# Depthwise taps kept in PSUM, normalising on ScalarE and a new order of work in the first phase of a fused block

## What is computed

```python
xn = layernorm(layernorm_over_channels(x)) * ln_w + ln_b
qkv = einsum('bchw,oc->bohw', xn, w_qkv)             # 576 channels
qkv = depthwise_conv_3x3(qkv, w_dw, padding='SAME')  # nine taps a channel
q, k, v = split(qkv * spatial_interaction)
attn = softmax(normalise(q) @ normalise(k).T * temperature)  # 8 heads, over channels
x = x + project(attn @ v)
t = tokens(x)
x = x + top-2 of 4 experts (192 -> 768 -> 192, gelu) on layernorm(t)
```

## Time and profile before

| | |
|---|---|
| median of 3 runs | 2112.06 us |
| lowest and highest | 2107.52 and 2113.6 us |
| the profiled execution | 2107.51 us |
| its span in the trace | 2105.4 us |
| first phase, within it | 0 to 723 us |
| busy over the span: TensorE, VectorE, ScalarE, GpSimd | 89%, 71%, 58%, 57% |

### The profile page before, as it was taken

The page is one execution under the profiler, slowest core; times in us unless marked ns, Lnnn a source line. Parts: engine busy times, 40 slices in busy tenths (PEclk is TensorE's granted clock), DMA queues, the critical chain, the costliest instruction groups (busy, mean ns, idle before and its releaser), DMA issues.

```text
span 2105.4 us, 35846 instructions
## 1 busy us (share of the span) xinstructions
PE 1864.8 (89%) x9782; PEld 1506.2 (72%) x9782; DVE 1484.8 (71%) x3474; ACT 1224.5 (58%) x2340; POOL 1196.4 (57%) x1083
## 2 busy tenths in 40 slices
PE   5698888888868499959899999999999999999966
PEld 3355555555545376748898998989989888888854
DVE  4799999999978754756667667676686755555633
ACT  3455656655645344426566666666666767666632
POOL 3656666656665500257766767666676776444420
PEclk9899999999988799979999999999999999999987
DMA  4343222223233268878788888878887787666659
GB/s 125 101 125 89 74 73 88 73 74 88 66 90 89 74 187 281 254 246 241 199 227 219 217 224 220 224 217 221 221 224 210 202 243 200 177 164 176 153 147 352
DMA packets 254466, 361.97 MB, mean 172 GB/s; under 512 B 27496, under 2 KB 184040, under 8 KB 254312
## 3 DMA queue, kind: packets, MB, share of 16 engines
q1 hardware_dynamic: 191656, 278.59, 44.3%
q0 software_dynamic: 50880, 60.59, 14.4%
q10 hardware_dynamic: 11776, 20.98, 2.9%
HBM read 222.76 MB, written 137.30 MB: 171 GB/s over the span
## 4 chain that ended last, share of the span: by engine, by line
PE 53%; DMA 4%; POOL 3%; DVE 2%; issue 2%; ACT 1%; SPq 0%; POOLq 0%; ACTq 0%; DVEq 0%
PE bank L1768 20%; PE bank L1784 14%; PE bank L1785 6%; PE bank L1751 6%; PE bank L1811 4%; PE bank L1803 3%; DMA xn<-acc_scratch 3%; POOL xs_scratch L1212 2%; POOL acc_scratch L1227 1%; DMA vc_scratch<-yo 1%; PE bank L1833 0%; DMA acc_scratch<-yo,tix 0%; DVE hl L1722 0%; ACT L1278 0%; DVE stat L1397 0%
## 5 line engine op out<-in xcount | busy, mean ns | idle before, releaser
L1227 POOL DMA_INDIRECT acc_scratch<-yo,tix x268 | 438.1, 1635 | 304.8 <-DVE yo L1609 242.7
L1768 PE MATMUL bank<-x_all,w1b 128*128 128x512 f32 x2010 | 548.8, 402 | 1.0 <-ACT hf L1278 1.0
L1784 PE MATMUL bank<-w_hl,hh 128*128 x1608 | 495.5, 360 | 7.1 <-DVE hl L1722 6.1
L1278 ACT ACTIVATE hf<-bank,b_col 128x512 f32<-128x512 f32 x402 | 276.7, 688 | 335.5 <-PE bank L1768 335.5
L1722 DVE TENSOR_TENSOR hl<-hf,hh 128x512 fp32r<-128x512 f32 x402 | 277.1, 690 | 270.4 <-ACT hh L1281 270.1
L1785 PE MATMUL bank<-w_hl,hl 128*128 x1608 | 404.7, 252 | 0.0
L601 DVE SCALAR_TENSOR_TENSOR acc<-zwin,wdw,acc 128x512 f32<-128x512 f32 (+2 forms) x462 | 401.5, 909 | 2.6
L1768 PEld LDWEIGHTS bank<-x_all,w1b 128*128 128x128 f32 x2010 | 348.1, 188 | 55.2 <-ACT hf L1278 1.4
L1784 PEld LDWEIGHTS bank<-w_hl,hh 128*128 128x128 f32 x1608 | 301.9, 188 | 41.7 <-issue 11.0
L1785 PEld LDWEIGHTS bank<-w_hl,hl 128*128 128x128 f32 x1608 | 306.0, 190 | 17.4
L1212 POOL DMA_INDIRECT xs_scratch<-xn,idx x256 | 262.4, 1025 | 85.5 <-issue 75.6
(11 more groups left out here) (259 smaller groups left out, 2935.1 us busy)
## 6 DMA issues: line engine op xcount, KB each, us to landing
w1b<-w1s_scratch SPq DMA_DIRECT2D x134, 768.0 KB, 5.0
xs<-xs_scratch SPq DMA_DIRECT2D x67, 522.0 KB, 6.0
xtok_scratch<-xtok SPq DMA_DIRECT2D x32, 384.0 KB, 2.7
v_scratch<-zv SPq DMA_DIRECT2D x64, 192.0 KB
vc_scratch<-yo ACTq DMA_DIRECT2D x64, 192.0 KB, 3.7
vd<-vc_scratch SPq DMA_DIRECT2D x64, 192.0 KB
xtok<-xtok_scratch SPq DMA_DIRECT2D x32, 384.0 KB, 7.0
acc_scratch<-x SPq DMA_DIRECT2D x32, 384.0 KB, 5.5
```

Of the source, the lines that this page charges most:

```text
L1227: nc.gpsimd.indirect_dma_start(acc_dram, bass.IndirectOffsetOnAxis(ap=tix[:, J % 4, t:t + 1], axis=0), yo[:, J % YN, t, :], None, compute_ ...
L1278: nc.scalar.activation(hf[:, k % 3, :], lb[k % 2][:, :], ACT.Gelu, bias=b1_col[:, bass.ds(exp_of[J] * CH + k, 1)]).then_inc(gelu, 1)
L1768: last = nc.tensor.matmul(lb[k % 2][:, :], w[:, q, :], v[:, J % 2, :], start=(i == 0), stop=(i == 4))
L1784: nc.tensor.matmul(yb[t][:, 0:2 * C], hh[:, k % 3, cols], w, start=(k == 0), stop=False, skip_group_check=True)
```

## The change

The taps of VectorE now read and write the PSUM bank; only the last tap of a channel tile writes `acc`, and only that one waits until GpSimd has taken the block before. With it, `dw` on TensorE waits until the whole chain that used the same bank is done, and no longer for its first tap. Normalising goes to ScalarE as scale and bias of four activations; VectorE makes the bias `nb` = -mean x 1/std, one operation of 128 x 4. TensorE makes the first taps of the next convolution, `dw(i, 0)`, between z's fourth and fifth tile and no longer at the start of the next step, and `gram(m, 3)` comes behind z's third tile. ScalarE spreads the squares and puts the copies of q and k, the ninth tap and the copies of z in another order. VectorE does four taps of tile 0 first (`HEAD_START`), then one, then four of tile 1 one after the other; the aggregates of the statistics come before two taps of tile 2.

```diff
@@ -48,7 +48,7 @@
 POOL_TAP = 8
-HEAD_START = 3
+HEAD_START = 4
 CX = C + E
@@ -174,6 +174,7 @@
             small = sb(p1, "small", [128, 6, ROWS])
+            nb = sb(p1, "nb", [128, ROWS])
             gw = sb(p1, "gw", [128, 2, E])
@@ -224,7 +225,7 @@
             r_link, r_ok = sem("r_link"), sem("r_ok")
-            tn_ok, tn_dup = sem("tn_ok"), sem("tn_dup")
+            nb_ok, tn_ok, tn_dup = sem("nb_ok"), sem("tn_ok"), sem("tn_dup")
             ac_t = sem("ac_t")
@@ -510,21 +511,26 @@
                     n = i - 2
-                    if n.within(0, NB):
-                        lo, hi = slots(n)
-                        for ct in range(QK):
+
+                    def square(ct):
+                        if n.within(0, NB):
+                            lo, hi = slots(n)
                             act.wait_ge(qs_ok, QK * n.val + ct + 1)
...
                                                  ACT.Square, accum_out=nrm[:, ct, bass.ds(n.val, 1)]).then_inc(sq_ok, 1)
-                        copy_q(n, 0)
-                    if (i - 1).within(0, NB):
-                        act.wait_ge(z_a, 5 * min(i.val, NB) if i.static else 5 * i.val)
-                        act_tap(i - 1, 0)
-                    if n.within(0, NB):
-                        copy_q(n, 1)
-                    if (i - 1).within(0, NB):
-                        act_tap(i - 1, 1)
+
+                    def row_q(t):
+                        if n.within(0, NB):
+                            copy_q(n, t)
+
+                    def tap(ct):
+                        if (i - 1).within(0, NB):
+                            act_tap(i - 1, ct)
+
+                    row_q(0)
+                    square(0)
+                    row_q(1)
                     b = i + 2
@@ -532,22 +538,40 @@
                                 wait(act, tn_ok, b.val - 1)
+                                wait(act, bn_ok, b.val - 1)
                             nc.scalar.activation(xtok[:, b.par, 2 * k:2 * k + 2, 0:CA],
...
                                                  ACT.Copy).then_inc(xt_a, 1)
-                    if n.within(0, NB):
-                        copy_q(n, 2)
-                        copy_q(n, 3)
                     if (i - 1).within(0, NB):
-                        act_tap(i - 1, 2)
+                        act.wait_ge(z_a, 5 * min(i.val, NB) if i.static else 5 * i.val)
+                    tap(0)
                     if i.within(0, NB - 1):
-                        for ct in range(4):
-                            copy_z(i, ct)
-                    if (i + 1).within(0, NB - 1):
-                        act.wait_ge(tn_ok, (i + 1).val + 1)
+                        copy_z(i, 0)
+                    row_q(2)
+                    square(1)
+                    if i.within(0, NB - 1):
+                        copy_z(i, 1)
+                    row_q(3)
+                    tap(1)
+                    if i.within(0, NB - 1):
+                        copy_z(i, 2)
+                    tap(2)
+                    if i.within(0, NB - 1):
+                        copy_z(i, 3)
+                    a = i + 1
+                    if a.within(0, NB - 1):
+                        act.wait_ge(nb_ok, a.val + 1)
+                        wait(act, ac_t, 2 * a.val)
+                        act.wait_ge(xt_a, 2 * a.val + 2)
+                        for t in range(ROWS):
+                            last = nc.scalar.activation(tn[:, t, 0:C], xtok[:, a.par, t, 0:C], ACT.Identity, bias=nb[:, t:t + 1],
+                                                        scale=rs_all[:, bass.ds(a.val * ROWS + t, 1)])
+                        last.then_inc(tn_ok, 1)
+                        act.wait_ge(tn_ok, a.val + 1)
                         nc.scalar.activation(tn[:, :, C:256], tn[:, :, CA:C], ACT.Copy).then_inc(tn_dup, 1)
+                    square(2)
                     if i.within(0, NB - 1):
@@ -590,17 +614,17 @@
                     ky, kx = divmod(DVE_TAPS[ct][k], KX)
-                    a = acc[:, ct, lo:hi, :]
+                    bank = db[(n.par + ct) % 2][:, lo * W:hi * W].rearrange("p (r w) -> p r w", w=W)
                     if k == 0:
-                        wait(dve, qs_ok, QK * (n.val - 1) + ct + 1)
                         dve.wait_ge(dw_t, QK * n.val + ct + 1)
-                        before = db[(n.par + ct) % 2][:, lo * W:hi * W].rearrange("p (r w) -> p r w", w=W)
                     else:
                         dve.wait_ge(dw_l[ct], n_dve[ct] * n.val + k)
-                        before = a
+                    last = k == n_dve[ct] - 1
+                    if last:
+                        wait(dve, qs_ok, QK * (n.val - 1) + ct + 1)
                     nc.vector.scalar_tensor_tensor(
-                        out=a, in0=zwin[n.par][:, ct, ky + lo:ky + hi, kx:kx + W],
-                        scalar=wdw[:, ct, DVE_TAPS[ct][k]:DVE_TAPS[ct][k] + 1], in1=before, op0=ALU.mult, op1=ALU.add).then_inc(dw_l[ct], 1)
+                        out=acc[:, ct, lo:hi, :] if last else bank, in0=zwin[n.par][:, ct, ky + lo:ky + hi, kx:kx + W],
+                        scalar=wdw[:, ct, DVE_TAPS[ct][k]:DVE_TAPS[ct][k] + 1], in1=bank, op0=ALU.mult, op1=ALU.add).then_inc(dw_l[ct], 1)
 
@@ -616,13 +640,9 @@
                     if has_n:
-                        for k in range(n_dve[0] - HEAD_START):
+                        tap(n, 0, HEAD_START)
+                        for k in range(4):
                             tap(n, 1, k)
-                            tap(n, 0, k + HEAD_START)
-                        for k in range(n_dve[0] - HEAD_START, n_dve[1]):
-                            tap(n, 1, k)
-                            if k + 1 < n_dve[1]:
-                                tap(n, 2, k - (n_dve[0] - HEAD_START))
                     if b.within(0, NB - 1):
@@ -630,16 +650,15 @@
                     if has_n:
+                        for ct, k in ((1, 4), (2, 0), (1, 5), (2, 1), (2, 2)):
+                            tap(n, ct, k)
+                    if a.within(0, NB - 1):
+                        wait(dve, tn_ok, a.val)
+                        dve.wait_ge(r_ok, 2 * a.val + 2)
+                        nc.vector.scalar_tensor_tensor(out=nb[:, :], in0=mv[:, a.par, :, 0], scalar=-1.0,
+                                                       in1=rs_all[:, bass.ds(a.val * ROWS, ROWS)], op0=ALU.mult, op1=ALU.mult).then_inc(nb_ok, 1)
+                    if has_n:
                         tap(n, 2, 3)
-                    if a.within(0, NB - 1):
-                        wait(dve, ac_t, 2 * a.val)
-                        dve.wait_ge(r_ok, 2 * a.val + 2)
-                        for t in range(ROWS):
-                            last = nc.vector.tensor_scalar(tn[:, t, 0:C], xtok[:, a.par, t, 0:C], mv[:, a.par, t, 0:1],
-                                                           rs_all[:, bass.ds(a.val * ROWS + t, 1)], ALU.subtract, ALU.mult)
-                        last.then_inc(tn_ok, 1)
-                    if has_n:
-                        tap(n, 2, 4)
                     if b.within(0, NB - 1):
@@ -647,6 +666,7 @@
                     if has_n:
+                        tap(n, 2, 4)
                         tap(n, 2, 5)
@@ -699,7 +719,7 @@
                         last_n, last_ct = (n, 0) if ct == 2 else (n - 1, ct + 1)
-                        pe.wait_ge(dw_l[last_ct], n_dve[last_ct] * last_n.val + 1)
+                        pe.wait_ge(dw_l[last_ct], n_dve[last_ct] * (last_n.val + 1))
                     for k, tap in enumerate(PE_TAPS[ct]):
@@ -750,8 +770,6 @@
                     has_i, has_n, has_m = i.within(0, NB - 1), n.within(0, NB), m.within(0, NB)
-                    if has_n:
-                        dw(n, 0)
                     if has_i:
@@ -792,10 +810,15 @@
                         gram(m, 2)
+                    if has_i:
+                        z(i, 2)
+                    if has_m:
                         gram(m, 3)
                     if has_i:
-                        z(i, 2)
                         z(i, 3)
+                    if i.within(0, NB):
+                        dw(i, 0)
+                    if has_i:
                         z(i, 4)
```

## The result

The changed kernel takes **2003.95 us** (median of four runs, 2002.25 to 2004.87), the kernel before 2110.36 beside it (2107.52 to 2113.6). The ratio is 0.949, with a 95% interval of 0.948 to 0.951. The forecast was 2012 with a range of 1996 to 2058. The profiled execution took 2004.87 us with a span of 2003.1; before it was 2107.5 and 2105.4, so the span lost 102.3 us.

What follows compares the result with a forecast made beforehand. VectorE was taken to bound the first phase at 19.9 us a step; with TensorE the new bound, 16.6 + 0.1 + 0.2 = 16.9, saving 75 us plus 25 elsewhere: 2012 us, range 1996 to 2058.

Steps and rivals of the forecast that it cites:

- The level of the sum: Whole span: 75 us gained in 25 steady first-phase steps plus 25 us outside them, 100 us in all.
- the upper bound of +0.66 us: VectorE taps: extra price per tap if one PSUM bank cannot be read and written at once; forecast took 0.
- the loop: ScalarE's work between z's fourth tile and the next transposes: 3.3 us against TensorE's 3.6, fitting by 0.3.
- `nb` at 0.1 us: VectorE's added 128x4 operation for the normalising bias, priced at about 0.1 us a step.
- The step's start is level; I add 0.1: Step's start: transposes to `x_c` take 2.9 us, TensorE's other work meanwhile also 2.9; 0.1 us added.
- TensorE's own work: TensorE's step without its idle times: 19.27 us less the waits gives 16.6 us, the new bound.
- The clock: Steady stretch: stretches at a granted clock of 0.59 cost 0.2 us a step, left in the forecast.
- New waits eat a part: Rival: ScalarE's activations, the step's start and DVE writes add 1.2 us a step; 2047 us, chance 0.18.
- Contention stays: Rival: POOL also holds up taps in PSUM, DVE's step 17.9 us; 2062 us, chance 0.05.
- slower in place: Rival: one bank cannot be read and written in one pass, DVE's step 24.5 us; about 2245 us, chance 0.06.
- Better than the sum: Rival: the low-clock stretches go and POOL runs freely, 16.4 us a step; 1998 us, chance 0.07.
- The signs: Changed profile: taps near 745 ns, DVE under 92% busy waiting for `xh_a`, duplicate done before the last z tile.

Runs made afterwards that it cites:

- The experiment: Changed kernel with normalising back on VectorE, its four operations placed two taps earlier in the queue than in the run of 2045.2 us: 2007.0 us.
- the two kernels of the second set: Changed kernel with three taps of tile 0 before `x_c`, not four: 1997.2 us; the same with `dw(n, 2)` behind z's first tile: 1988.0 us.
- the first set: Changed kernel with taps in `acc` 2077.8 us, normalising on VectorE 2045.2, first taps at the step's start 2036.1; kernel before with taps in PSUM 2103.9.
- the first three kernels: Changed kernel with taps in `acc`: 2077.8 us; kernel before with only taps in PSUM: 2103.9; changed kernel with normalising on VectorE: 2045.2.

## Why the prediction was right, step by step

*The level of the sum.* Steady steps: 75 us forecast, 497 - 421 = 76 measured. 33 to 117 us: 11 forecast, 84.4 - 72.6 = 11.8 measured. The two steps behind the steady ones: 9 forecast, 11.2 measured. The end of the phase: 7 forecast, 5.8 measured. The start loses 1.0 (1.5 forecast) and the second phase 1.7 (0 forecast). In all the span lost 102.3 us for a forecast of 100. Of the 8 us between 2012 and the measured median, that explains 2.6; the other 5.5 come from where the profiled executions lie: mine was 4.6 below its median, the changed kernel's 0.9 above.

*Taps in PSUM.* Right. A tap costs 750 ns, the upper bound of +0.66 us is excluded, and the contention is gone (750 against 927). With `nb` taken off, VectorE's step is 371.4 / 25 = 14.9 us; the forecast had 15.2 for it. The rule of the Trainium skill ("Perfetto Trace Analysis", Optimizing Scalar/DVE Operations) that PSUM costs a VectorE instruction some 65 ns more than SBUF isn't borne out here: 750 ns with PSUM in and out, 745 with PSUM in only, and 746 to 747 for each of the four taps at 439.69 with all in SBUF.

*Normalising on ScalarE.* The price was right: 535 ns for a forecast of 500, and the loop fits by 0.55 us and not 0.3. By the Trainium skill's 93 ns for each operand from memory ("ScalarE: Activation LUTs", What ACT_TABLE_LOAD costs) it would be 0.53 us as an estimate, and the trace's 535 ns agree. Why it pays was only half seen. I counted 2.3 us a step off VectorE's sum. The experiment shows that it isn't the sum that counts but the collision, and that another place in the queue does as well.

*`nb` at 0.1 us.* **Mis-sized**: 1.14. I had seen that an operation with two SBUF inputs is held up beside GpSimd and had priced it by its size all the same; 0.15 us is its price with GpSimd idle. It cost nothing, as its removal shows, because VectorE waits for TensorE anyway.

*TensorE's order.* "The step's start is level; I add 0.1" was the step of the working that failed, if with a small price. I followed the loop from the transposes through `xh_a`. `xh_a` is there at 359.3 (ScalarE writes it from 358.68 on, for 0.59 us), but `xl_a` starts at 359.98: it waits in VectorE's queue behind four taps. I hadn't counted that `HEAD_START` puts one more of them in front. It costs 0.46 us a step, as the two kernels of the second set show, 16.82 to 16.36.

On the other side, TensorE's own work was taken too long. Counted as the forecast counts it, by starts, the wait marked 0.47 is 0.64 us: the input transposes start 0.75 us behind the matmul ahead of them, where 0.11 is the distance without a wait. So the own work is 16.77 - 0.64 = 16.1 us and not 16.6. Half of the difference is a fourth wait in the very step of the kernel before that the forecast read. The matmul's row doesn't mark it; that of its weight load does:
```profile
439.66 0.27 PE L778 MATMUL bank<-ident,xc_b 128*128 128x128 f32 x1
440.01 0.31 PEld L721 LDWEIGHTS bank<-ident,qs 128*128 128x128 f32 x3 [0.33 <-ACT qk_tok L469]
440.02 0.55 PE L721 MATMUL bank<-ident,qs 128*128 128x128 f32 x3
```
The second transposing of q starts 0.36 us behind the matmul ahead of it, 0.10 in the changed kernel (362.05 to 362.15): 0.25 us of waiting for ScalarE's copy of q, which the forecast counted as work. The other 0.2 lies right behind the waits, where the next matmuls start some 0.06 us later than elsewhere, and in the last wait, 0.83 us from start to start for a forecast of 0.77.

*The clock.* I left 0.2 us a step in for stretches at a granted clock near 0.6. They are gone, 1.00 over the whole stretch. In the kernels here whose steps are all alike the clock is 1.00 throughout, also where TensorE waits in five places for 2.7 us a step (taps in PSUM alone); in those whose steps differ it falls to 0.85 to 0.92 in some of the long ones. What decides it the runs don't settle.

So the step came out right by luck in part. Its three errors, +0.54 for the wait at the start (0.64 for 0.1), -0.47 for the own work and -0.2 for the clock, nearly cancelled: 16.9 forecast, 16.77 measured.

*The rivals.* New waits eat a part: only the 0.46 us of `x_c`. Contention stays and slower in place: excluded by the taps' 750 ns. The price of the former didn't add up: a step of 17.9 instead of 16.9 is 25 us more and not 50, about 2037 and not 2062. Better than the sum: its condition, no stretches at a low clock, came true, but the wait for `x_c` took the rest.

*The signs.* Some that the forecast named didn't come: VectorE was busy for 94% and not under 92 (`nb`); what it waited for was TensorE's first taps, 14.6 us in 25 steps, and `xh_a` once, 0.8 us; and ScalarE's duplicate ended 1.0 us behind the start of z's last tile (374.11 against 373.11), not before it. Taps with none over 800 ns, normalising near 0.5 us and GpSimd's add at 1.30 us and no longer 1.66 did come.

*What the forecast got by luck.* It added up the parts as if each gave its share. They don't: PSUM alone 7 us, the order alone -8 (one run each, both near the noise of 6), PSUM with the order 65 (2110 to 2045), all three 106. The sum over the engines' work in the final state came out, with errors that cancelled, while a forecast for any one part by the same sum was not, as three of the four expectations of the first set show: the first three kernels came out slower than they said.

## What to carry to other kernels

When you take work off the engine that is the bound, first follow each ring of waits with the new durations; until its order is changed as well, the step may stay as long as it was. An operation that collides with GpSimd is best priced by its place: look whether GpSimd rests at that moment, and move it by a tap or two before moving it to another engine. Where all else is balanced, count what stands in the queue ahead of the one operation that others wait for, here a single tap in front of `x_c`.

## What the runs showed of the hardware

A 128x4 operation of VectorE with two SBUF inputs waits out a GpSimd add of 1.30 us (1.27 against 0.15 us). The normalising operation, with one SBUF tensor in and one out, is held up as well: four of 128x192 take 1.24 us with GpSimd resting and 3.29 us beside its add and multiply. The statistics over the same tensor (L650, 345 ns each) are not: four take 1.13 us beside GpSimd's add too. Nor are taps whose third operand is in PSUM, not one over 758 ns of 398. GpSimd pays as well: its 128x512 multiply takes 1.28 us in the changed kernel and 1.62 us where the taps are in `acc`. All of this agrees with a rule of the Trainium skill ("SBUF — State Buffer", Who interferes with whom), which would have priced `nb` rightly: a VectorE operation with two SBUF inputs shares a read path with GpSimd, the second of the two to start is blocked until the first is done, a tensor-scalar operation can take the shared path too, and others with one SBUF input don't. One row leaves open who counts as the second: beside GpSimd's multiply at 304.30 the operation that waited starts at 304.26 in the trace. Reading and writing the same PSUM bank in one VectorE operation costs nothing that can be seen (750 against 745 ns).
